# Probabilities times values in two column halves, each behind one half of a step of scores

## The reference

```python
x = x + _L0_attn_a_ref(_layernorm(x), ...)   # 16 heads of 16, a bias by position, causal
x = x + _L0_ffn_ref(...)                      # experts, three more blocks between
...
x = x + _L1_attn_a_ref(_layernorm(x), ...)   # 16 query heads, 4 key/value heads, rotated q and k, not causal
...
scores = einsum('bhqd,bhkd->bhqk', q, k) / sqrt(16)
p = softmax(scores, axis=-1)
ctx = einsum('bhqk,bkhd->bqhd', p, v)
return ctx @ Wout.T
```

## Time and profile before

| | |
|---|---|
| median of 3 runs | 1539.38 us (1537.95 to 1543.03) |
| profiled execution, its own time | 1539.91 us |
| span of its trace | 1538.1 us |
| mean granted TensorE clock | 0.952 of full |
| TensorE busy | 1373.5 us, 89% |
| VectorE busy | 1089.9 us, 71% |
| ScalarE busy | 619.8 us, 40% |

### The profile page before, as it was taken

How to read it: one execution, slowest core, us unless ns; L and a number is a source line. 1 busy time by engine, 2 the same in 40 slices (tenths; PEclk the granted TensorE clock), 3 DMA queues, 4 the chain that set the end, 5 groups by cost and what they waited for, 6 DMA issues and landing times. The chain is left out here.

```text
span 1538.1 us, 20758 instructions
## 1 busy us (share of the span) xinstructions
PE 1373.5 (89%) x7632; PEld 968.4 (63%) x7632; DVE 1089.9 (71%) x2216; ACT 619.8 (40%) x1156; POOL 327.1 (21%) x291
## 2 busy tenths in 40 slices
PE   4799999879999989899977999999799889889797
PEld 4455555568888878788861333323477668678676
DVE  5766666698679478787648666777476578888765
ACT  2254555543333333343222555665632343334221
POOL 4311100073433213333322040300022001021010
PEclk9799999999999999999976999999999899999899
DMA  7828330300000000000043250400000000000000
GB/s 153 96 31 111 43 43 2 120 10 1 1 1 1 1 1 1 1 1 1 1 52 52 49 80 28 67 2 1 1 0 1 0 1 0 1 1 1 14 14 28
DMA packets 32320, 39.05 MB, mean 25 GB/s; under 512 B 6003, under 2 KB 27227, under 8 KB 32091
## 3 DMA queue, kind: packets, MB, share of 16 engines
q1 hardware_dynamic: 32218, 37.73, 14.7%
HBM read 14.45 MB, written 2.10 MB: 11 GB/s over the span
## 5 line engine op out<-in xcount | busy, mean ns | idle before, releaser
L1402 DVE TENSOR_REDUCE attn_negm<-ps 128x2 f32<-128x1024 f32 (+3 forms) x256 | 260.1, 1024 | 95.0 <-PE ps L987 52.8
L1221 ACT ACTIVATE attn_probs<-ps 128x512 f32<-128x512 f32 (+3 forms) x512 | 235.5, 516 | 148.0 <-PE ps L1019 77.1
L501 POOL TENSOR_TENSOR moe_h_low<-expert_h,moe_h_high 128x512 fp32r<-128x512 f32 x96 | 138.6, 1445 | 277.2 <-ACT moe_h_high L446 277.2
L1011 PE MATMUL ps<-attn_qs,attn_ks 99*128 99x512 bf16 (+4 forms) x512 | 149.9, 350 | 22.5 <-ACT attn_probs L1221 12.4
L987 PE MATMUL ps<-attn_ks,attn_qs 96*128 96x512 bf16 (+4 forms) x512 | 143.6, 365 | 17.4 <-DVE attn_negm L1402 14.7
L464 ACT ACTIVATE moe_silu<-ps 128x512 f32<-128x512 f32 x96 | 57.5, 599 | 203.0 <-PE ps L366 202.7
L1849 PE MATMUL ps<-sb_f_down,tail_h 128*128 128x256 f32 x512 | 123.5, 387 | 7.1 <-DVEq L2140 7.1
L1032 PE MATMUL ps<-attn_probs,attn_va 128*32 128x512 f32 (+3 forms) x1024 | 118.3, 534 | 0.7 <-ACT attn_probs L1221 0.6
L1011 PEld LDWEIGHTS ps<-attn_qs,attn_ks 102*128 102x128 bf16 (+1 forms) x512 | 43.7, 98 | 116.2 <-ACT attn_probs L1221 84.6
L1849 PEld LDWEIGHTS ps<-sb_f_down,tail_h 128*128 128x128 f32 x512 | 98.7, 194 | 24.3 <-DVEq L2140 7.3
L2113 DVE TENSOR_TENSOR tail_h<-tail_silu,ps 128x512 f32<-128x512 f32 x64 | 43.5, 681 | 84.6 <-PE ps L1839 53.9
(11 more groups left out here) (354 smaller groups left out, 3241.8 us busy)
## 6 DMA issues: line engine op xcount, KB each, us to landing
attn_qs<-attn_part SPq DMA_DIRECT2D x96, 128.0 KB, 4.6
attn_ks<-attn_part SPq DMA_DIRECT2D x48, 128.0 KB, 7.2
out_x<-x SPq DMA_DIRECT2D x4, 512.0 KB, 2.6
attn_ks<-attn_part SPq DMA_DIRECT2D x24, 64.0 KB, 4.4
x<-in_x SPq DMA_DIRECT2D x2, 512.0 KB, 4.3
x<-in_x SPq DMA_DIRECT2D x1, 1024.0 KB, 7.5
moe_raw<-in_f_down SPq DMA_DIRECT2D x2, 512.0 KB, 6.4
sb_f_gate<-in_f_gate SPq DMA_DIRECT2D x2, 512.0 KB, 4.2
```

Of the source, the lines that this page charges most:

```text
L501: pool.tensor_tensor(hc.low[:, j % RING, :], h[:, j % RING, :], hc.high[:, j % RING, :], ALU.subtract).then_inc(low_done, 1)
L1011: last = pe.matmul(ps[:, bank, 0:width2(kt)], ks[0:ROWS2, b % 2, hd % KH, kt * P:(kt + 1) * P], qs[0:ROWS2, b % 2, hd, T - width2(kt):T], ...
L1221: act.activation(pr[:, s2 % RING, j, 0:n], ps[:, p2_bank[UNIT * s2 + j], 0:n], ACT.Exp, scale=HD ** -0.5).then_inc(exp_done, 1)
L1402: dve.tensor_reduce(m, ps[:, 2 * half:2 * half + 2, 0:width1(qt)], AX, ALU.max, negate=True).then_inc(r1_free, 1)
```

## The change

`context` takes a second argument, `part`. It multiplies only half of the columns of the step, the left half for part 0, the right half for part 1. Part 0 is issued behind the first half of the scores, ahead of the `middle` jobs; part 1 behind the second half, ahead of the `end` jobs. The accumulation's start flag is set by part 0 of a unit's first step alone; `pv_done` is raised by part 1 alone, as before once a step. The number of context products doubles, from 4 to 8 a step, and their columns together stay the same.

```diff
-            def context(s3):
+            def context(s3, part):
                 u, kt = s3 // NT, s3 % NT
                 b = u // 4
+                wide = width2(kt) // 2
+                left = T - width2(kt) + part * wide
                 pe.wait_ge(exp_done, UNIT * (s3 + 1))
-                if kt == 0:
+                if kt == 0 and part == 0:
                     at_least(pe, ctx_out, u)
                     job = ("values", b, VJ - 1)
                     pe.wait_ge(free[jobs.freed_by[job]], jobs.count[job])
                 for j in range(UNIT):
                     hd = UNIT * (u % 4) + j
-                    last = pe.matmul(ps[SLOT * j:SLOT * (j + 1), CTX, T - width2(kt):T], va[:, b % 2, kt, hd % KH, :],
-                                     pr[:, s3 % RING, j, 0:width2(kt)], start=kt == 0, stop=kt == NT - 1,
+                    last = pe.matmul(ps[SLOT * j:SLOT * (j + 1), CTX, left:left + wide], va[:, b % 2, kt, hd % KH, :],
+                                     pr[:, s3 % RING, j, part * wide:(part + 1) * wide], start=kt == 0 and part == 0, stop=kt == NT - 1,
                                      skip_group_check=True)
-                last.then_inc(pv_done, 1)
+                if part == 1:
+                    last.then_inc(pv_done, 1)
...
                         scores1(2 * s1 + half)
                         if causal:
                             masks1(2 * s1 + half)
-                    if half == 0:
-                        for job in middle:
-                            do(job)
-                if 0 <= s3 < STEPS:
-                    context(s3)
-                for job in end:
-                    do(job)
+                    if 0 <= s3 < STEPS:
+                        context(s3, half)
+                    for job in (middle, end)[half]:
+                        do(job)
```

## The result

The changed kernel takes 1527.51 us (median of 6 runs, 1525.84 to 1530.64), the kernel before 1537.75 beside it (6 runs, 1535.71 to 1543.03). The ratio is 0.993, with a 95% interval of 0.9913 to 0.9946: 0.7% faster. The forecast was 1527.5, 0.8% under the first median of 1539.4. That the two times agree to the last digit is luck: the saving forecast was 11.9 us and the measured one is 10.2 (the interval of the ratio makes it 8.3 to 13.4), and the median beside the change happened to lie 1.6 lower than the first one.

The account below looks back on a forecast made before the run. TensorE was taken to set the pace in the second attention while waiting for the exponentials. Savings of 10.4 us there and 1.5 in the first attention, 11.9 together, took 1539.4 to 1527.5 us; range 1522 to 1533 (0.66).

Parts of the forecast that it names:

- TensorE waits for the exponentials inside a step, and half a context fits there: Plain step, second attention: 0.54 us of waits before work that would fit into them; step 3.38 to 3.06.
- Price of a switch 0.23: Each added context group, both attentions: 0.23 us fixed whatever its width; 128 more groups cost 29 us if nothing covers them.
- The terms of the second attention: Its context steps: 21 plain save 0.32 each, 13 flip 0.44, 11 maxima 0.15, 16 others pay 0.23; sum -10.4 us.
- The 8 steps with jobs in the middle: Second attention, steps with projections or values in the middle: no wait to fill, so each pays 0.23 us.
- The one wait that moves forward: Step after a unit's last context: part 0 needs ScalarE's copy, done at +0.73, part ready at +0.96; 0.23 us to spare.
- The first attention gains in its flip steps alone: First attention: 14 steps save 0.42 us each, 5.9; 19 with middle jobs or in the drain pay 0.23; sum -1.5.
- The wide steps before them: First attention, the wide step before a flip step: its shorter end is given back at once; 0 gain, 10 times.
- The 18 narrow steps: First attention, steps with narrower passes: wait about as long as the price; taken as 0, bounds -0.2 and +0.23 us each.
- Pass 2's wait for the exponentials under 15 us in the second attention: Sign to look for: this wait of TensorE's loads falls from 55 us to under 15.
- The other sign: Second attention: no row of TensorE waiting for the exponentials outside the first steps.
- VectorE close behind but not binding: Second attention, four steps: VectorE needs 11.8 us, TensorE 12.9; VectorE stays behind by 1.1.
- that rival: VectorE or ScalarE sets the second attention's pace; four steps stay at 13.7, not 12.9; 1536.5 us; chance 0.15.

Follow-up runs that it names:

- the mixed kernel: Against the kernel before, each step takes its own order: context whole at the end, whole behind the first half of the scores, or cut in two; 1512.46 us, ratio 0.9844.

## Why the prediction was right

- *TensorE waits for the exponentials inside a step, and half a context fits there.* Shown: the plain step went from 3.38 to 3.08 (forecast 3.06), and where the cut was made without the move nothing was gained.
- *Price of a switch 0.23, on a line from 128 to 512 columns, 0.26 for a half of 64.* Shown: 0.24 where it was added alone, 0.01 where the added group needed no switch. The 256-column halves take 0.57 to 0.58, as forecast. The 64-column halves of the first attention take 0.25:

```profile
224.50 0.32 PE L1034 MATMUL ps<-attn_probs,attn_va 128*32 128x64 f32 x8
224.75 0.84 PE L1011 MATMUL ps<-attn_qs,attn_ks 102*128 102x512 bf16 x2
```

- *The terms of the second attention*, as the differences of step lengths between the two traces: 21 steps without flip or maxima -6.3 (forecast -6.7), 13 with a flip -5.2 (-5.7), 11 with the maxima -1.4 (-1.7). A half is 1.54 and not 1.53, and three of the flip steps, behind a step with outputs, took 3.86 before where I had put 4.00 for all. The 8 steps with jobs in the middle cost 1.3 (forecast 1.8), if the one that a slow stretch of the clock had hit before (8.96, now 7.61) is set to its alike's 7.37. That stretch, 1.6, is part of the 11.4 gained and no effect of the cut that I can show; behind the attentions 1.3 were lost again. The drain cost 1.2 (forecast 1.8), and the stretch up to the end of the third context step 0.6 (forecast nothing). Without the clock's 1.6 the second attention gains 9.8, against 10.4.
- *The one wait that moves forward, part 0 behind the copy: "No wait, 0.23 to spare".* Wrong in four of the 13 flip steps of the second attention. Six have the 0.23, and three behind output products have 2.05. In the four behind a step that ends with rows or a projection, ScalarE has another copy of 0.60 to do first, for that job. The copy of the context then ends 1.28 or 1.34 after the step's start instead of 0.73, and part 0 stands idle for 0.35 or 0.40 until it is done:

```profile
861.80 0.59 ACT L1178 ACTIVATE attn_ctxs<-ps 128x512 f32<-128x512 f32 x1
862.49 0.64 PE L1034 MATMUL ps<-attn_probs,attn_va 128*32 128x256 f32 x8 [0.35 <-issue]
```

The first attention has eight with 0.17 (forecast 0.16), three behind outputs with more and two that wait 0.55. The prediction had named this wait as a sign of being wrong; it read one flip step and took it for all. The forecast survives it because the same copy had held these steps before as well (second half at +1.83 or +1.88, not +1.27): each is 0.43 or 0.44 shorter all the same, as the others are. In the drain no pass 1 stands in between; there the prediction had looked only at the exponentials, and allowed 0.1:

```profile
1060.60 0.60 PE L1011 MATMUL ps<-attn_qs,attn_ks 99*128 99x512 bf16 x2
1061.43 0.64 PE L1034 MATMUL ps<-attn_probs,attn_va 128*32 128x256 f32 x8 [0.23 <-issue]
```

```profile
1060.73 0.60 ACT L1178 ACTIVATE attn_ctxs<-ps 128x512 f32<-128x512 f32 x1
```

The context starts 0.83 after the step's start instead of 0.53, just behind the copy's end at 1061.33. It is 0.3 us in this step, and 0.1 to 0.2 in each of two steps in the drain of the first attention.

- *The first attention gains in its flip steps alone.* Nearly: 13 of them -5.0 (forecast 14 x 0.42 = 5.9). The one of the earlier trace rows takes 3.49 where the forecast was 3.44. The fourteenth, in the drain, became 0.1 longer. The wide steps before them, counted as zero, gave 0.9 together, and the two sums are one effect, as the hold of the second score product can be booked on either side of the step's start. The 18 narrow steps, taken as zero, gave 0.3 together. Jobs in the middle cost 2.1 (forecast 2.8), the drain 1.1 with its flip step (forecast 1.2), the first steps 0.7 (forecast nothing). So the 2.3 gained against 1.5 forecast is a sum of misses in both directions.
- *Pass 2's wait for the exponentials under 15 us in the second attention.* Wrong as a sign, not as a cause:

```profile
PEld ps L1011 <- ACT attn_probs L1221: 25.0, 65, 0.4
```

It counts the idle time of the weight loads, which ends at a semaphore while the stream of products still runs: the pairs span 0.60 with no gap between. Such a row overstates what TensorE loses; the lengths of pairs and steps don't. The other sign held: in the loop of the second attention, first steps and drain left out, TensorE's products waited 5.9 us in 14 places for the exponentials before, and nowhere after.
- *VectorE close behind but not binding.* Right, with 0.31 idle in each half of 1.54. The price of that rival was mis-set, though: it lets four steps "stay" at 13.7, while the rows give 3.38 + 4.00 + 3.38 + 3.38 = 14.1 before.

## What to carry to other kernels

When an engine waits in a fixed place of a loop, look for work of the same turn that can be moved into the wait whole, and cut it only where nothing whole fits: the move without the cut gained as much here (0.9924 against 0.993), and choosing for each step what to move gained twice as much (0.9844). Price a cut from groups of different widths, where the part that doesn't shrink is the intercept, and ask whether it belongs to the group or to the switch before and after it. Read the gain from the lengths of the steps, kind by kind; totals of waits mix in idle time that costs nothing.

## What the runs showed of the hardware

- A group of products with 32 weight columns between products of 128 costs 0.24 us once, whatever its width from 64 to 512 columns; a second group right behind costs 0.01.
- A single bf16 product with 48 weight columns holds the next one for 0.17 us; with its weights filled up to 128 columns, for 0.06. Its own weight load takes 0.10 either way. A change between fp32 and bf16 at 128 columns costs nothing that shows: in the mixed kernel the flip's four fp32 products stand 0.44 from start to start of their neighbours, 0.11 each (1009.89 to 1010.33).
